# Local attention with 64 queries by 128 keys, scores on two row tiles, and layer norms in bursts of four

## The reference

```
h = shift_token(x)                       # half of the features come from the position before
q, k, v = split(h @ wqkv, 3)             # 8 heads of 64
q, k = l2norm(q) * qs, l2norm(k) * ksc   # norm over 64, then rotary tables
o = local_attention(q, k, v)             # window 64: query i sees keys i-64 .. i
x = x + o @ wo
h = layer_norm(shift_token(x)) * g + b
x = x + gated_gelu(h) @ w2 + b2
```

## Time and profile before

| | |
|---|---|
| median of three runs | 2253.29 us (2249.87 to 2253.87) |
| the profiled execution | 2256.39 us, of which the span from first to last instruction is 2254.6 us |
| PE, PEld busy in the span | 89%, 55% |
| DVE, ACT, POOL busy | 58%, 72%, 23% |
| local attention, first and second layer | 1116.0 to 1581.5 us, 1684.0 to 2149.0 us |
| cross attention, about | 215 to 1088 us |

### The profile page before, as it was taken

The page is one execution under the profiler, slowest core; times in us unless marked ns, Lnnn a source line. Parts: engine busy times, 40 slices in busy tenths (PEclk is TensorE's granted clock), DMA queues, the critical chain, the costliest instruction groups (busy, mean ns, idle before and its releaser), DMA issues. The chain is left out here.

```text
span 2254.6 us, 68002 instructions
## 1 busy us (share of the span) xinstructions
PE 2007.2 (89%) x27900; PEld 1250.2 (55%) x27900; DVE 1304.6 (58%) x3762; ACT 1631.0 (72%) x2732; POOL 512.4 (23%) x357
## 2 busy tenths in 40 slices
PE   8888999999999999999868888888886888888988
PEld 5764555555555555555346556666334566566633
DVE  4445333333333333330379998997537999998754
ACT  4333799999899999999547777777434777777743
POOL 1004000000000000000255555552005555555200
PEclk9997899999999999999868888889996888888999
DMA  1001111111111111110200000000000000000000
GB/s 50 3 3 55 64 57 62 52 53 60 52 52 56 58 52 63 52 37 3 85 1 1 0 0 0 0 0 1 0 0 0 1 1 0 0 0 0 0 5 33
DMA packets 32077, 57.06 MB, mean 25 GB/s; under 512 B 5328, under 2 KB 26704, under 8 KB 31824
## 3 DMA queue, kind: packets, MB, share of 16 engines
q1 hardware_dynamic: 31824, 53.34, 6.8%
HBM read 21.35 MB, written 2.10 MB: 10 GB/s over the span
## 5 line engine op out<-in xcount | busy, mean ns | idle before, releaser
L672 ACT ACTIVATE x_probs<-x_pss 128x1024 f32<-128x1024 f32 x832 | 806.6, 1021 | 52.5 <-PE x_pss L593 37.7
L607 PE MATMUL x_acc<-x_probs,x_v 128*32 128x256 f32 x6656 | 437.9, 381 | 0.0
L593 PE MATMUL x_pss<-x_qx,x_kx 32*128 32x256 bf16 x9984 | 350.0, 271 | 11.0 <-ACT x_probs L672 4.2
L593 PEld LDWEIGHTS x_pss<-x_qx,x_kx 32*128 32x128 bf16 x9984 | 222.3, 93 | 198.2 <-ACT x_probs L672 181.4
L1183 ACT ACTIVATE prob<-l_sim,l_neg_top,l_inv_norm 128x192 f32<-128x192 f32 (+1 forms) x512 | 259.9, 509 | 90.0 <-DVE l_neg_top L1083 88.9
L876 POOL TENSOR_TENSOR l_turned_half<-l_raw,l_tabB 128x512 f32<-128x512 f32 x128 | 223.6, 1768 | 445.5 <-ACT l_raw L1147 445.5
L955 PE MATMUL l_pss<-l_kT,qz 128*128 128x192 f32 (+1 forms) x1024 | 206.7, 339 | 114.1 <-DVE l_top L1077 114.1
L955 PEld LDWEIGHTS l_pss<-l_kT,qz 128*128 128x128 f32 x1024 | 166.3, 210 | 178.7 <-DVE l_top L1077 151.2
L607 PEld LDWEIGHTS x_acc<-x_probs,x_v 128*32 128x32 f32 x6656 | 206.5, 110 | 92.9 <-issue 8.7
L719 DVE COPY x_vnext<-x_psp 128x128 f32<-128x128 f32 (+1 forms) x199 | 59.2, 298 | 317.4 <-PE x_psp L571 312.1
L648 POOL COPY x_zq<-zT 128x256 f32 (+1 forms) x15 | 6.0, 401 | 771.0 <-PE x_psp L578 690.4
(11 more groups left out here) (178 smaller groups left out, 2948.5 us busy)
## 6 DMA issues: line engine op xcount, KB each, us to landing
x_kx<-x_kp SPq DMA_DIRECT2D x96, 208.0 KB, 2.3
x_cT<-in_context SPq DMA_DIRECT2D x16, 832.0 KB, 5.8
x_qx<-x_qp SPq DMA_DIRECT2D x48, 192.0 KB, 2.3
xT<-in_x SPq DMA_DIRECT2D x8, 256.0 KB, 5.1
out_x<-xT SPq DMA_DIRECT2D x8, 256.0 KB, 2.1
w_wqkv<-in_f_wqkv SPq DMA_DIRECT2D x2, 768.0 KB, 4.8
w_w<-in_f_w SPq DMA_DIRECT2D x2, 384.0 KB, 3.4
w_wo<-in_f_wo SPq DMA_DIRECT2D x2, 256.0 KB, 4.9
```

What stands on the lines that cost most here:

```text
L593: ins = pe.matmul(pss[bank(k, 2 * p + r // 2)][:, r % 2, e, :], kx[par][rows, g, j * P:(j + 1) * P], qx[par][rows, g, a * S:(a + 1) * S], ...
L607: ins = pe.matmul(acc[32 * r:32 * r + 32, 0:S], v[:, j, g, r, :], probs[SLOT[p]][r // 2][:, r % 2, e, :], start=(u == 0), stop=(u == UNITS ...
L672: act.activation(probs[SLOT[p]][y][:, :, :, :], pss[bank(k, 2 * p + y)][:, :, :, :], ACT.Sigmoid, scale=HD ** -0.5).then_inc(weighed, 1)
```

## The change

In the local attention:

- A turn has two blocks b of 128 queries instead of six units, each with two portions h of four heads. In block 1 each run of 64 queries gets its own 128 keys: queries 128 to 191 take keys 64 to 191, queries 192 to 255 take keys 128 to 255. All score tiles are 128 by 128.
- Scores read only the 64 rows of their head, in pairs on rows 0 to 63 and 64 to 127, which write to two banks. The zero-padded qz is replaced by qT.
- The values of positions 64 to 191, which the middle keys need, are made by two SBUF to SBUF transfers (vmid).
- The shifted input comes by two transfers from SP, four sequences ahead, no longer by DVE.
- ACT no longer copies the values, DVE does; the 1/norm is Exp(-0.5 Ln(x)) on ACT and one Newton step on DVE.
- The hand-written orders are new, and the skew between portions is smaller.

In the norms: two banks for the mean, eight buffers for squares, variances and spreads in bursts of four, one table set preloaded, the Newton step in two instructions.

The core of the diff, with "..." where lines are left out:

```diff
-    UNIT = [(0, (0, 1, 2, 3)), (0, (4, 5, 6, 7)), (1, (0, 1)), (1, (2, 3)), (1, (4, 5)), (1, (6, 7))]
-    KEYS = [(0, P), (WINDOW, S)]
+    KEYS = [[(0, P, 0, P)], [(WINDOW, WINDOW + P, 0, WINDOW), (P, S, WINDOW, P)]]
...
+            def shift(n):
+                if n >= 4:
+                    sp.wait_ge(v_projected, 2 * n - 6)
+                sp.dma_start(hs[n % 4][0:64, :], zT[0:64, n * S:(n + 1) * S]).then_inc(landed[n % 4], 16)
+                sp.dma_start(hs[n % 4][64:P, 1:S], zT[64:P, n * S:(n + 1) * S - 1]).then_inc(landed[n % 4], 16)
+            def middle(n):
+                sp.wait_ge(v_ready, 2 * n + 2)
+                if n >= 2:
+                    sp.wait_ge(valued, 2 * n - 2)
+                sp.dma_start(vmid[n % 2][0:64, :], vt[n % 2][64:P, 0, :]).then_inc(mid_landed[n % 2], 16)
+                sp.dma_start(vmid[n % 2][64:P, :], vt[n % 2][0:64, 1, :]).then_inc(mid_landed[n % 2], 16)
...
+            def score(x, b):
+                    for p in range(PH):
+                        for lo, hi, first, last in KEYS[b]:
+                            for e in range(2):
+                                rows = slice(64 * e, 64 * e + 64)
+                                ins = pe.matmul(pss[e][first:last, p, :],
+                                                qT[r % 2][rows, p, b * P + first:b * P + last],
+                                                kT[r % 2][rows, p, lo:hi], start=True, stop=True)
...
+            def turn(x):                      # PE
+                project_qk(later(x, 2), 0)
+                project_out(later(x, -1))
+                turn_over(x, 0, 0)
+                project_qk(later(x, 2), 1)
+                turn_over(x, 0, 1)
+                score(x, 1)
+                value(x, 0)
+                flip(later(x, 1), 0)
+                project_v(later(x, 1), 0)
+                turn_over(x, 1, 0)
+                flip(later(x, 1), 1)
+                turn_over(x, 1, 1)
+                project_v(later(x, 1), 1)
+                score(later(x, 1), 0)
+                value(x, 1)
...
+            def turn(x):                      # DVE
+                mask(x, 0, 0)
+                mask(x, 0, 1)
+                norm(x, 0, 0)
+                add(later(x, -1))
+                straight_part(later(x, 2), 0)
+                norm(x, 0, 1)
+                mask(x, 1, 0)
+                mask(x, 1, 1)
+                sums(later(x, 2), 0)
+                straight_part(later(x, 2), 1)
+                norm(x, 1, 0)
+                copy_v(later(x, 1), 0)
+                place_keys(later(x, 1), 0)
+                sums(later(x, 2), 1)
+                norm(x, 1, 1)
+                floor_of(later(x, 2))
+                place_keys(later(x, 1), 1)
+                copy_v(later(x, 1), 1)
+                inverse_norms(later(x, 2))
...
+            def turn(x):                      # ACT
+                exps(x, 0, 0)
+                copy_qk(later(x, 2), 0)
+                exps(x, 0, 1)
+                copy(x, 0, 0)
+                squares(later(x, 2), 0)
+                copy(x, 0, 1)
+                copy_qk(later(x, 2), 1)
+                copy_out(x, 0)
+                exps(x, 1, 0)
+                squares(later(x, 2), 1)
+                exps(x, 1, 1)
+                place_queries(later(x, 1), 0)
+                copy(x, 1, 0)
+                place_queries(later(x, 1), 1)
+                copy(x, 1, 1)
+                roots(later(x, 2))
+                copy_out(x, 1)
+            act.preload_act_table_set("natural_log_exp_and_others")
```

POOL's turn keeps its work: both halves of the turned product with their sums, then both scalings of keys. In the norm:

```diff
+            def variances(g):
+                pe.wait_ge(square_ready, base + 4 * g + 4)
+                for c in range(4):
+                    ins = pe.matmul(var[g][32 * c:32 * c + 32, :], ones_mean[:, 0:32], square[4 * g + c][:, :],
+                                    start=True, stop=True)
+                ins.then_inc(var_ready, 1)
...
+            variances(0)
+            for n in range(6, NCH):
+                mean_of(n)
+            variances(1)
+            keep_warm(WARM)
+            widen(0)
+            keep_warm(WARM)
+            widen(1)
...
+            refine(0)
+            scale(0)
+            scale(1)
+            refine(1)
+            for n in range(2, NCH):
+                scale(n)
```

More of the change, by code:

```diff
@@ L36 @@
 NEG = -3.0e38
-class Own:
-    def __init__(self, eng, sem, per):
-        self.eng, self.sem, self.per, self.base, self.n = eng, sem, per, 0, 0
-    def turn(self, i):
-        assert self.n in (0, self.per), (self.n, self.per)
-        self.base, self.n = i * self.per, 0
-    def step(self, ins):
-        ins.then_inc(self.sem, 1)
-        self.n += 1
-        return self.n
-    def wait(self, n=None):
-        self.eng.wait_ge(self.sem, self.base + (self.n if n is None else n))
 def layer_norm(nc, tag, norms, src, dst, loads=(), zeros=(), gain=None, source=None,
@@ L234, in _ @@
                 act.activation(rsquare[g][:, :], rstd[g][:, :], ACT.Square).then_inc(guess_ready, 1)
+            act.preload_act_table_set("natural_log_exp_and_others")
+            for n in range(6):
+                square_of(n)
+            guess(0)
+            for n in range(6, NCH):
+                square_of(n)
+            guess(1)
 def retention(nc, zT, w, vb):
@@ L1171, in copy_out @@
-            def copy_out(n, b):
-                if exists(n):
-                    act.wait_ge(valued, n * NSU + (4, 6)[b])
-                    at_least(act, out_ready, n)
-                    act.activation(oT[:, 2 * b:2 * b + 2, :], pso[:, 2 * b:2 * b + 2, :], ACT.Copy).then_inc(o_ready, 1)
-            def exps(n, u, s):
-                if not exists(n):
-                    return
-                (blk, heads), r = UNIT[s], s % 2
-                act.wait_ge(negated, n * NSU + s + 1)
-                for m, h in enumerate(heads):
-                    ins = act.activation(probs_of(s)[:, m, :], scores_of(sim[r], s)[:, m, :], ACT.Exp,
-                                         bias=neg_top[r][:, m:m + 1], scale=inv_norm[u][:, blk, h:h + 1],
-                                         accum_out=total[r][:, m:m + 1])
-                ins.then_inc(exped, 1)
@@ new lines, in exps @@
+            def exps(x, b, h):
+                if exists(x):
+                    n, r, _ = x
+                    c = 4 * n + 2 * b + h
+                    act.wait_ge(negated, c + 1)
+                    at_least(act, turned, c - 3)
+                    for head in range(HALF * h, HALF * h + HALF):
+                        ins = act.activation(prob[b][:, head, :], sim[b][:, head, :], ACT.Exp,
+                                             bias=neg_top[b][:, head:head + 1], scale=inv_norm[r % 2][:, b, head:head + 1],
+                                             accum_out=total[b][:, head:head + 1])
+                    ins.then_inc(exped, 1)
@@ new lines, in copy, with turn @@
+            def copy(x, b, h):
+                if exists(x):
+                    n, _, _ = x
+                    act.wait_ge(turned, 4 * n + 2 * b + h + 1)
+                    at_least(act, valued, 2 * n + b - 1)
+                    act.activation(probT[b][:, HALF * h:HALF * h + HALF, :], pst[h][:, :, :], ACT.Copy).then_inc(copied, 1)
+            def turn(x):
+                exps(x, 0, 0)
[15 more added lines that the diff above has]
+                copy_out(x, 1)
```

579 lines of the change are left out of this document (248 added, 331 removed).

## The result

The changed kernel takes 2114.8 us, the median of four runs (2109.33 to 2121.37), beside 2253.58 for the kernel before in as many: a ratio of 0.9378, 95% interval 0.9334 to 0.9422. It is 139 us faster. The forecast, 2200 us, had the sign, and the range (2110 to 2265) just holds the time, but the saving is 2.6 times the one foretold. The profiled execution took 2109.33 us, its span 2107.5 us against 2254.6 before: 147 us less to account for.

The account below looks back on a forecast made before the run. No engine was full; a ring of waits between engines bound the turn, 26.4 us instead of 27.3. Turns, fill and drain save 36.8 us, norms 21: 58 off 2256.4 gives 2198.6, stated as 2200, range 2110 to 2265.

Parts of the forecast that it names:

- the ring: Local attention: engines wait for each other in a closed chain, giving a turn of 26.4 us instead of 27.3.
- a hold by POOL's second addition: Local attention, block 1, between DVE's inverse and norm: DVE waits 2.3 us for POOL.
- The first rival: Local attention: engines' sums decide, POOL and DVE fall into step differently, turn 21.5 to 23 us, kernel 2065; chance 0.17.
- DVE's own work: Local attention: DVE's instructions in one turn sum to 15.9 us without waits for POOL.
- 4.6 us of holds: Local attention: time DVE instructions lose per turn to POOL's, within bounds of none and 8 us.
- transposes, value projection, scores of block 0: Last part of the ring: 0.55 + 0.95 + 1.1 + 0.15, and 0.5 for PE's lower clock, 3.2 us.
- Scores of block 1: Local attention on PE: sixteen half-row products take half of the single price, 1.9 us instead of 3.8.
- The clock: Local attention: PE, idle for about 5 us, comes back at the lower clock, costing 0.5 us a turn.
- The norms: Five layer norms: each 4 to 5 us shorter, 21 us less in all, bounds 12 and 30.
- Fill and drain: Start and end of each local attention layer: 4 us less per layer, bounds 0 and 8.
- the rival of reloads: Local attention on ACT: Ln and Exp reload tables in the loop, kernel 2230 to 2280 us; chance 0.06.
- The rival of a ring longer than before: Local attention: half-row scores don't overlap and PE runs at the lower clock, turn 29.3 us, kernel 2288; chance 0.15.

Follow-up runs that it names:

- a2: Changed kernel with four one-column memsets on DVE between the second straight part and the norm behind it: 2173.27 us.
- b1: Changed kernel with POOL's instructions in the local attention cut to four columns each, all waits kept: 2050.14 us.
- a3: Changed kernel with score products reordered, all of rows 0 to 63 first, then all of rows 64 to 127: 2124.31 us.
- c1: Changed kernel with both 12 filler products on PE ahead of block 1's first transposes and scores one row tile after the other: 2118.09 us.
- a4: Changed kernel with 12 filler products on PE in its idle time ahead of block 1's first transposes: 2073.87 us.
- a1: Changed kernel with the five layer norms of the kernel before: 2148.19 us.
- e1: Changed kernel with 12 filler products on PE ahead of block 1's first transposes and DVE's first straight part ahead of its addition: 2042.05 us.

## Why the prediction was right in sign and wrong in size

**The failed step** is in the ring: "inverse 0.2, a hold by POOL's second addition 2.3, norm 0.6: 3.1". It measured 0.81. The prediction names no reason why POOL's second addition should come first; I had let it because it waits only for the straight part, while DVE has an inverse to do in between. But the straight part ended at 1279.20 + 1.21 = 1280.41, POOL began 0.14 us behind that, and DVE, whose inverse had begun at 1280.33 under the straight part's tail, began the norm 0.12 behind it. I could not have read such a margin out of the rows of before; it should have been two cases, 2.3 us a turn apart (a2: 58 us in all), and not one term of the sum. The first rival, POOL and DVE falling into step in another way, at 2065 us, had this mechanism; the result lies between it and the forecast. DVE's own work was forecast well, 15.9 us a turn, which is what b1 shows; of the 4.6 us of holds that I took (4.2 are placed in the ring), b1 finds 2.2.

The ring's other terms, forecast against the turn from 1264.58 to 1288.25 (23.67 us):

| term | forecast | measured |
|---|---|---|
| masks to the exponents' start | 2.2 | 1.7 |
| exponents, raw copy, exponents | 5.0 | 4.8 |
| to the second norm's end, with two holds | 2.3 | 2.2 |
| transposes, scores of block 1 | 2.65 | 2.0 |
| masks, sums, straight part | 4.7 | 5.1 |
| inverse, hold, norm | 3.1 | 0.8 |
| copies and sums | 2.35 | 2.3 |
| second inverse and norm | 0.9 | 0.8 |
| transposes, value projection, scores of block 0 | 3.2 | 3.9 |

They add up to 26.4 and, before rounding, 23.7. Without the missing hold the sum is 24.1, 0.4 from what was measured. Eight of nine terms are within 0.7 us, which supports the ring as the mechanism. That their sum is so near is in part luck: six are together 1.6 us too long and two together 1.1 too short.

**Scores of block 1** were second: 1.9 us taken, 1.03 measured. The earlier trace rows had shown 13 ns a record; I allowed only half of the single price. Sixteen products on `64*64` tiles hold PE for 64 ns each, less than a third of the 0.22 of a full one (0.89 us for eight records in the earlier trace rows, from 1312.16 to 1313.05; the forecast used 0.24), and 100 when neighbours lie on the same row tile. a3 and c1 show what is lost without the overlap of the row tiles: 1.1 us for both blocks, 44 us in the time with what the clock adds.

**The clock** went the other way: 0.5 us taken for PE's slow return, 1.3 measured by a4. It reaches flips, transposes and value projection, and there the forecast was 0.7 short (last line of the table).

**The norms** gave 33 us (a1) instead of 21, above the bound of 30. In the norm before the first layer, 4.6 us was forecast and 7.6 came. From the last centering on, it is 11.9 us instead of 17.6 (12.9 forecast), of which 0.64 is the variance burst. The other 1.9 us lies ahead of the last centering (8.7 us instead of 10.7 from the first mean), where the forecast took nothing: there the old norm ran its first means at a granted clock of 0.59 (1087.8 to 1091.5) and the new one at 1.00. Why the clock differs there stays open; in a1 the old norm's first ten mean records last 6.23 us again.

**Fill and drain**: 4 us a layer taken; the stage less sixteen turns went from 28.9 to 409.0 - 382.9 = 26.1, 2.8 a layer.

**Right**: DVE idles for 5.8 us of a steady turn (5 to 6 forecast); value and shift transfers have no waiter in the turns, but PE's 4.2 us at the layer's start is one; no table load between the norms' starts (one at 1067.85, one at 1088.82, none in the turns; L1155 and L1157, the roots, last 0.22 us and 0.23). The Trainium skill, ScalarE: Activation LUTs, section Table sets: the hidden batching unit, has both functions in one set, which this trace now bears out; the rival of reloads fell. The rival of a ring longer than before fell with the scores' overlap. The shift's copies on DVE were not put back and the smaller skew was not undone, so what each of these is worth by itself stays open.

## What to carry to other kernels

Where two engines exclude each other, write down who comes first at each meeting point and by how much; a meeting decided by a few hundredths of a microsecond is two forecasts, not a term, even if the chip then decides it in the same way in every turn. Before counting removed work as a gain, cut the other engine's instructions to a few columns: here DVE's busy time then fell by 6 us of a 27 us turn, all of it waiting inside instructions, and the turn by as much. Look at the granted clock of both kernels before comparing them. On a ring like this one, PE's idle time is paid twice, as a wait and as a lower clock behind it; a few products without use in the gap returned 41 us, and with one addition moved by one place 73 (e1).

## What was not expected of the hardware

Before, all turns measured agreed within 0.05 us; after, with the same instructions in each, they vary from 23.47 to 24.45. Why stays open. Products of fp32 on `64*64` tiles of alternating rows and columns come every 64 ns, on one row tile at a time every 100, where a full product of 128 columns held PE for 0.22 us in the stage before; on `64*128` tiles the figures are 0.136 and 0.205. And four memsets of one column, which delay a norm by 0.04 us, cost 58 us in a kernel of 2115.
